# Sixteen-head attention: where the products for the row maxima stand among scores and values

## The chip, the cores and the metric

One core of one Trainium2 chip runs one program. The metric is the device time of one execution in microseconds (us), as the median of the runs. The engines: PE is TensorE (matmuls; PEld its weight loads), DVE is VectorE, ACT is ScalarE, POOL is GpSimd, SP is SyncE, which issues the DMAs here.

## The reference, cut to what matters

The program is a two-layer block on x (8 x 512 x 256) with a context of 8 x 1601 x 256. The change touches the first cross-attention alone, of 16 heads with 16 dimensions each:

```
v = (values @ Wv.T).reshape(N, -1, H, Dh)     # N = 8, 1601 keys, H = 16, Dh = 16
k = (keys @ Wk.T).reshape(N, -1, H, Dh)
q = (query @ Wq.T).reshape(N, -1, H, Dh)      # 512 queries
energy = jnp.einsum('nqhd,nkhd->nhqk', q, k)
attn = jax.nn.softmax(energy / jnp.sqrt(jnp.float32(EMBED_DIM)), axis=3)
out = jnp.einsum('nhql,nlhd->nqhd', attn, v).reshape(N, -1, H * Dh)
```

Behind it come four experts, a second attention with one wide head, and a memory layer with product keys; they stay as they are.

## The kernel before

`attend_heads` (L333) works through 32 units, `unit(b, g)` (L530): one of 8 batches, one group of four heads. The scores of a head are taken keys by queries, 128 keys at a time, so that one unit has 13 tiles of keys (`KT`) times four heads (`HG`) = 52 score products of up to 128 x 512 (`scores`, L506), as many exps on ScalarE (`exps`, L585) and as many value products (`values`, L515), which add up in one PSUM bank over the unit, each head in 32 of its partitions. Queries and keys are held as bf16 parts, six of them stacked in the rows of `qs` and `ks`, and three more rows carry minus the row's maximum, so that the exp needs no bias.

Those maxima have to be known a unit ahead. So, beside the work of unit u, TensorE computes rough scores of unit u + 1 (and, from step 10 on, of unit u + 2), queries by keys, and VectorE takes their maxima. That is `max_product` (L485), 32 jobs (`NJ`) of a pair of matmuls each, one for either head of two, with up to 401 columns; the two matmuls use rows 0 to 63 and 64 to 127 of the array. A reduction (L650) follows each pair. When all 32 are reduced, VectorE takes the maxima of the partial maxima (L654), TensorE turns them (`turn_max`, L501, called at step `TURN_AT` = 10), VectorE splits them in three bf16 parts (`split`, L632 to L640, in the order of VectorE's work ahead of reduction 0), and SP copies these into the rows of `qs` (`rows_out`, L408), which the first scores of the next unit wait for (L545). The transposed maxima lie in the second buffer of the maxima, so job 1 waits for the split (L493).

The order on each engine is written out by hand and each runs its own queue in order. On TensorE, the loop of steps (L542) goes from kt = 1 to 13: a step issues the four scores of key tile kt (in step 13 the first four of the next unit) and the four values of tile kt - 1. `plan` (L355) says at which places of a step the pairs stand: the number j means ahead of score j, so 3 is ahead of the last of the four, and `HG` = 4 is behind the last; "values" is behind the four values. Six steps (`THREE`, L351) have three pairs, the other seven two.

PSUM has eight banks: three for scores (`SBANKS`), one for the sum of the values, and two buffers of two banks for maxima (`MBANKS`). The waits that matter are two: a score waits for the exp three before it (L511), and a pair of maxima waits for the reduction of the pair two before it:

```
pe.wait_ge(m_red, u * NJ + n + 1)                 # L495; m_red starts at MBANKS = 2
```

VectorE has one more duty in the loop: the inversion of the sums of the unit before, in three pieces (`invert`, L619: a transposition L626, a reciprocal L628, a transposition L630), ahead of the reductions that `INVERT_AT` (L349) names. POOL divides with the result and spreads the values; ScalarE copies the sums out at the end of the unit (L598).

Of the kernel before, what the change touches and what calls it, by code (L numbers as in the profile page):

```python
# [28 lines left out]
KT = -(-KEYS // P)  # L29
H, DH = 16, 16  # L30
HG = 4
# [301 lines left out]
def attend_heads(nc, sem, t):  # L333
# [12 lines left out]
    SCALE = 1.0 / float(D) ** 0.5  # L346
    UNITS = B * G
    NLOAD = 2 * len(Q_PART) + 2 * MAX_PARTS
    INVERT_IN, INVERT_AT = 3, (16, 17, 21)  # L349
    TURN_AT = 10  # L350
    THREE = (1, 4, 6, 8, 11, 13)  # L351
    NJ = len(max_jobs)
    EARLY = sum(2 + (kt in THREE) for kt in range(TURN_AT, KT + 1))
    order = iter([*range(EARLY, NJ), *range(EARLY)])
    plan = {kt: {place: next(order) for place in ((2, HG, "values") if kt in THREE else (HG - 1, "values"))}  # L355
            for kt in range(1, KT + 1)}
    with Stage(nc, "at") as st:
        ks, qs = st.sb("ks", [STACK, SLOTS, HG, KEYS], BF16), st.sb("qs", [STACK, SLOTS, HG, S], BF16)
        kh, qh = st.sb("kh", [P, SLOTS, HG // 2, KEYS], BF16), st.sb("qh", [P, SLOTS, HG // 2, S], BF16)
# [24 lines left out]
        with nc.Block() as block:  # L384
# [60 lines left out]
            def _(pe):  # L445
# [39 lines left out]
                def max_product(b, g, u, n):  # L485

                    p, q, c = max_jobs[n]
                    a, w = MSPANS[c]
                    if n == 0:
                        pe.wait_ge(kq_in[g], b * 16 * NLOAD + 16 * NLOAD)  # L490
                    if n == 1:

                        pe.wait_ge(m_parts, u + 1)  # L493

                    pe.wait_ge(m_red, u * NJ + n + 1)  # L495
                    nc.tensor.matmul(ps_m[:, n % MBANKS, 0, 0:w], qs[0:MAX_ROWS, g, 2 * p, q * P:q * P + P],  # L496
                                     ks[0:MAX_ROWS, g, 2 * p, a:a + w], start=True, stop=True)
                    nc.tensor.matmul(ps_m[:, n % MBANKS, 1, 0:w], qh[MAX_ROWS:2 * MAX_ROWS, g, p, q * P:q * P + P],  # L498
                                     kh[MAX_ROWS:2 * MAX_ROWS, g, p, a:a + w], start=True, stop=True).then_inc(m_mm, 1)

                def turn_max(u):  # L501

                    pe.wait_ge(m_all, u + 1)
                    nc.tensor.transpose(turned_at, nmax[:, :], t["ident"][:, :]).then_inc(m_turned, 1)

                def scores(u, g, n):  # L506
                    kt, j = n // HG, n % HG
                    r = key_rows(kt)


                    pe.wait_ge(expd, u * NST + n + 1 + (SBANKS - 1 if g == n == 0 else 0))  # L511
                    nc.tensor.matmul(ps_s[0:r, (NST * g + n) % SBANKS, :], ks[:, g, j, kt * P:kt * P + r], qs[:, g, j, :],  # L512
                                     start=True, stop=True).then_inc(s_mm, 1)

                def values(u, g, n):  # L515
                    kt, j = n // HG, n % HG
                    r = key_rows(kt)

                    pe.wait_ge(expd, u * NST + n + 1 + SBANKS)
                    nc.tensor.matmul(ps_o[j * 32:(j + 1) * 32, :], vw[0:r, g % 2, kt * HG + j, :],  # L520
                                     pr[0:r, (NST * g + n) % PRING, :], start=kt == 0, stop=kt == KT - 1).then_inc(pv, 1)
# [8 lines left out]
                def unit(b, g):  # L530

                    u = b * G + g
                    nxt, over = ((b, x) if x < G else (b + 1, x - G) if b < last else None for x in (g + 1, g + 2))
                    def maxima(place, kt):

                        ahead, v = (nxt, u + 1) if kt < TURN_AT else (over, u + 2)
                        if place in plan[kt] and ahead is not None:
                            max_product(ahead[0], ahead[1], v, plan[kt][place])  # L540

                    for kt in range(1, KT + 1):  # L542
                        if kt == KT and nxt is not None:
                            pe.wait_ge(ones, nxt[1] + 1)
                            pe.wait_ge(m_in, u * 48 + 97)  # L545
                        for j in range(HG):
                            maxima(j, kt)
                            if kt < KT:
                                scores(u, g, kt * HG + j)
                            elif nxt is not None:  # L550
                                scores(u + 1, nxt[1], j)
                        maxima(HG, kt)
                        if nxt is not None and kt == TURN_AT:
                            turn_max(u + 1)
                        if kt == 1:
                            pe.wait_ge(v_wide, u + 1)

                            pe.wait_ge(acc_out, u + 1)
                        for j in range(HG):
                            values(u, g, (kt - 1) * HG + j)  # L560
                        maxima("values", kt)
# [6 lines left out]
                turn_max(0)  # L568
                for n in range(1, EARLY):
                    max_product(0, 1, 1, n)  # L570
                pe.wait_ge(k_out, len(halves))
                first_scores(0, 0)
                for b in range(B):
                    for g in range(G):
                        unit(b, g)
# [1345 lines left out]
def build(nc, ins, out, debug=None):  # L1921

    with ExitStack() as ctx:
# [59 lines left out]
        with nc.Block() as block:  # L1983
# [6 lines left out]
            def _(act):  # L1990
                act.wait_ge(t["consts"], 32)
                nc.scalar.activation(opened[:, :], gates[:, :], ACT.Tanh).then_inc(gates_opened, 1)
        project(nc, sem, t)
        attend_heads(nc, sem, t)
        stage_life.close()
        experts(nc, sem, t)
# [68 lines left out]
```

## Time and profile before

| | us |
|---|---|
| median of 3 runs (range) | 3662.23 (3660.39 to 3664.3) |
| the profiled execution | 3665.15 |
| its span, first to last instruction | 3663.4 |
| busy in it: TensorE matmuls | 3423.8 |
| VectorE | 2504.0 |
| ScalarE | 1513.7 |
| reductions of L650, 1024 of them | 974.3 |
| exps of L591, 1664 | 858.5 |
| scores of L512, 1664 | 524.1 |
| values of L520, 3328 (two for each value product) | 444.1 |
| maxima products, L496 and L498, 1024 each | 356.4 and 356.2 |

Matmuls are pipelined: a matmul's row may run on into the next one's, so the distance between starts, not the duration, tells what a matmul costs. In a row of the timeline a run of like instructions is merged: "x3" with 0.82 us is three, from the start of the first to the end of the last; where a stretch cuts a run, the row counts those up to the cut. What stands in brackets is the idle time of the engine ahead of the row and what ended it.

### The profile page before, as it was taken

To read this page: it belongs to the slowest core of one execution; us is meant where nothing else is said; L and a number is where in the kernel's file an instruction comes from. 1 tells how busy PE (TensorE), PEld (TensorE's weight loads), DVE (VectorE), ACT (ScalarE), POOL (GpSimd) and SP (SyncE) were. 2 spreads that over 40 slices of the span, in tenths; PEclk is the share of its full clock that TensorE was granted. 3 is DMA by queue.
4 is the path that set the end of the run, shared out by engine and by line. 5 is a ranking of instruction groups with operands and counts; after the bars stand their busy time and mean duration, and the time that the engine had idled before them with its cause. 6 is when DMAs were issued, how large, how long until landed. Compare 5 with 4: busy or idle time off the path is not lost. (4 is left out here: it accounts for less than half of the span.)

```text
span 3663.4 us, 63094 instructions
## 1 busy us (share of the span) xinstructions
PE 3423.8 (93%) x21900; PEld 2030.0 (55%) x21900; DVE 2504.0 (68%) x5808; ACT 1513.7 (41%) x2718; POOL 227.1 (6%) x251
## 2 busy tenths in 40 slices
PE   8979999999999999769977999987999999999999
PEld 5643222222222222258864545545889888989888
DVE  5538888888888888350013344438888888888885
ACT  4534777777777777512211222212222222222221
POOL 0021100000000000030000000000000000000000
PEclk9977999999999999979988999998999999999999
DMA  6687646455464552141120121212000000000000
GB/s 215 236 253 90 83 63 81 69 74 78 65 83 66 76 74 34 52 170 37 37 88 30 61 87 53 77 45 110 12 11 10 13 10 11 10 11 10 11 10 9
DMA packets 144167, 239.79 MB, mean 65 GB/s; under 512 B 22808, under 2 KB 100224, under 8 KB 143488
## 3 DMA queue, kind: packets, MB, share of 16 engines
q1 hardware_dynamic: 134768, 220.67, 28.4%
q0 software_dynamic: 4608, 12.59, 1.1%
q10 hardware_dynamic: 4624, 4.46, 0.4%
q8 instruction: 86, 1.41, 0.2%
q14 instruction: 81, 0.66, 0.1%
HBM read 170.38 MB, written 66.86 MB: 65 GB/s over the span
## 5 line engine op out<-in xcount | busy, mean ns | idle before, releaser
L650 DVE TENSOR_REDUCE at_pmax<-at_psm 128x2 f32<-128x800 f32 (+1 forms) x1024 | 974.3, 987 | 147.5 <-PE at_psm L498 128.8
L591 ACT ACTIVATE ring<-at_pss 128x512 f32<-128x512 f32 (+1 forms) x1664 | 858.5, 602 | 318.9 <-PE at_pss L512 318.9
L512 PE MATMUL at_pss<-at_qs,at_ks 99*128 99x512 bf16 (+1 forms) x1664 | 524.1, 387 | 16.8 <-ACT ring L591 8.1
L1653 PE MATMUL mt_psd<-mt_xl,mt_key_in 128*128 128x128 f32 x4096 | 491.0, 278 | 2.4 <-DMA mt_key_out<-m_out 2.4
L1653 PEld LDWEIGHTS mt_psd<-mt_xl,mt_key_in 128*128 128x128 f32 x4096 | 469.6, 193 | 3.8 <-DMA mt_key_out<-m_out 2.5
L1679 PE MATMUL mt_psu<-mt_key_out,mt_g 128*128 128x256 f32 x2048 | 447.4, 379 | 1.3 <-DVE mt_g L1889 1.3
L520 PE MATMUL at_pso<-ring,at_vw 128*32 128x512 f32 (+1 forms) x3328 | 444.1, 606 | 0.0
L496 PEld LDWEIGHTS at_psm<-at_ks,at_qs 64*128 64x128 bf16 x1024 | 95.1, 93 | 580.5 <-DVE at_pmax L650 351.3
L1679 PEld LDWEIGHTS mt_psu<-mt_key_out,mt_g 128*128 128x128 f32 x2048 | 386.7, 190 | 52.6 <-DVE mt_g L1889 1.4
L496 PE MATMUL at_psm<-at_ks,at_qs 64*128 64x400 bf16 (+1 forms) x1024 | 356.4, 348 | 20.5 <-DVE at_mpart L640 11.8
L498 PE MATMUL at_psm<-at_kh,at_qh 64*128 64x400 bf16 (+1 forms) x1024 | 356.2, 348 | 0.0
L1741 ACT ACTIVATE mt_g<-mt_psd 128x512 f32<-128x512 f32 x256 | 152.8, 597 | 351.3 <-PE mt_psd L1653 350.9
L512 PEld LDWEIGHTS at_pss<-at_qs,at_ks 99*128 99x128 bf16 (+1 forms) x1664 | 129.8, 98 | 264.5 <-ACT ring L591 154.8
L1889 DVE TENSOR_TENSOR mt_g<-mt_psc,mt_g 128x512 f32<-128x512 f32 x256 | 164.1, 683 | 55.8 <-PE mt_psc L1668 55.7
L1240 PE MATMUL aw_pss<-aw_ctxT,aw_gT 128*128 128x512 f32 (+1 forms) x512 | 187.6, 520 | 9.1 <-ACT aw_gT L1335 9.1
L1260 PE MATMUL aw_psw<-aw_pT,aw_ctx 128*128 128x512 f32 (+1 forms) x416 | 183.1, 594 | 0.8 <-issue 0.8
L1717 ACT ACTIVATE mt_sims<-mt_psx 128x512 f32<-128x512 f32 x64 | 38.2, 597 | 350.1 <-PE mt_psx L1626 350.1
L1395 DVE TENSOR_REDUCE aw_peak<-aw_pss 128x1 f32<-128x1601 f32 x32 | 58.4, 1825 | 175.9 <-PE aw_pss L1240 175.9
L1668 PEld LDWEIGHTS mt_psc<-mt_hot_w,mt_hot_m 128*128 128x128 f16 x4096 | 136.9, 98 | 36.2 <-issue 34.8
L1240 PEld LDWEIGHTS aw_pss<-aw_ctxT,aw_gT 128*128 128x128 f32 x512 | 91.3, 194 | 110.5 <-issue 98.8
L1859 DVE TENSOR_TENSOR mt_hot_m<-mt_iota_m,mt_picksT 128x2048 f16<-128x2048 f16 x128 | 150.2, 1214 | 0.0
L1357 ACT ACTIVATE aw_prob<-aw_pss,aw_shift 128x1601 f32<-128x1601 f32 x32 | 51.1, 1596 | 237.3 <-DVE aw_shift L1398 236.9
(218 smaller groups left out, 3792.3 us busy)
## 6 DMA issues: line engine op xcount, KB each, us to landing
at_ks<-k_dram SPq DMA_DIRECT2D x192, 200.1 KB, 6.7
k_dram<-pj_kp SPq DMA_DIRECT2D x24, 800.5 KB, 5.4
v_dram<-pj_v SPq DMA_DIRECT2D x8, 1664.0 KB, 9.1
at_vd<-v_dram SPq DMA_DIRECT2D x32, 416.0 KB, 10.7
pj_ctx<-ctxT SPq DMA_DIRECT2D x8, 1601.0 KB, 11.7
at_kh<-k_dram SPq DMA_DIRECT2D x128, 100.1 KB, 5.5
aw_ctxT<-ctxT SPq DMA_DIRECT2D x8, 1601.0 KB, 7.4
at_qs<-q_dram SPq DMA_DIRECT2D x192, 64.0 KB, 6.9
```

Of the source, the lines that this page charges most:

```text
L496: nc.tensor.matmul(ps_m[:, n % MBANKS, 0, 0:w], qs[0:MAX_ROWS, g, 2 * p, q * P:q * P + P], ks[0:MAX_ROWS, g, 2 * p, a:a + w], start=True, ...
L498: nc.tensor.matmul(ps_m[:, n % MBANKS, 1, 0:w], qh[MAX_ROWS:2 * MAX_ROWS, g, p, q * P:q * P + P], kh[MAX_ROWS:2 * MAX_ROWS, g, p, a:a + w] ...
L512: nc.tensor.matmul(ps_s[0:r, (NST * g + n) % SBANKS, :], ks[:, g, j, kt * P:kt * P + r], qs[:, g, j, :], start=True, stop=True).then_inc(s ...
L520: nc.tensor.matmul(ps_o[j * 32:(j + 1) * 32, :], vw[0:r, g % 2, kt * HG + j, :], pr[0:r, (NST * g + n) % PRING, :], start=kt == 0, stop=kt ...
L591: nc.scalar.activation(pr[0:r, (NST * g + n) % PRING, :], ps_s[0:r, (NST * g + n) % SBANKS, :], ACT.Exp, scale=SCALE).then_inc(expd, 1)
L650: nc.vector.tensor_reduce(pmax[:, 2 * p:2 * p + 2, q, c:c + 1], ps_m[:, n % MBANKS, :, 0:MSPANS[c][1]], AX.X, ALU.max).then_inc(m_red, 1)
L1240: ins = nc.tensor.matmul(ps_s[:, n, 0:w], gT[:, k, q * P:q * P + P], ctxT[:, s, k, a:a + w], start=k == 0, stop=k == KC - 1)
L1260: ins = nc.tensor.matmul(ps_w[:, m, :], ctx[0:r, kt, m * P:m * P + P], pT[0:r, s, kt, :], start=kt == 0, stop=kt == KT - 1)
L1653: ins = nc.tensor.matmul(ps_d[:, j % 2, y * P:y * P + P], key_in[:, k, j * YB + y, :], xl[:, s, k, :], start=k == 0, stop=k == KC - 1)
L1679: ins = nc.tensor.matmul(ps_u[:, 0:D], g[:, off % 2, y, :], key_out[:, y, :], start=y == 0, stop=y == YH - 1)
L1741: nc.scalar.activation(g[:, off % 2, j * YB:(j + 1) * YB, :], ps_d[:, j % 2, :].rearrange("p (y n) -> p y n", n=P), ACT.Gelu).then_inc(g_o ...
L1889: nc.vector.tensor_tensor(gv, ps_c[:, tb % CRING, h, :].rearrange("p (n u y) -> p y u n", u=2, y=YH), gv, ALU.mult).then_inc(w_out, 1)
```

## The change

The pairs of maxima are put at other places among scores and values, their numbers stay. Each step has two pairs back to back ahead of the third score (one in step 10), and seven steps, named in the new `THREE`, have another one behind the values. No pair stands between the scores and the values any more. With nine instead of ten pairs from step 10 on (`EARLY`), the three pieces of the inversion move by one reduction.

```diff
-    INVERT_IN, INVERT_AT = 3, (16, 17, 21)
+    INVERT_IN, INVERT_AT = 3, (17, 18, 22)
     TURN_AT = 10
-    THREE = (1, 4, 6, 8, 11, 13)
+    THREE = (2, 3, 5, 7, 8, 11, 13)
+    BETWEEN = 2
     NJ = len(max_jobs)
-    EARLY = sum(2 + (kt in THREE) for kt in range(TURN_AT, KT + 1))
+
+    def pairs_at(kt):
+
+        return {BETWEEN: 1 if kt == TURN_AT else 2, "values": int(kt in THREE)}
+
+    EARLY = sum(sum(pairs_at(kt).values()) for kt in range(TURN_AT, KT + 1))
     order = iter([*range(EARLY, NJ), *range(EARLY)])
-    plan = {kt: {place: next(order) for place in ((2, HG, "values") if kt in THREE else (HG - 1, "values"))}
-            for kt in range(1, KT + 1)}
+    plan = {kt: {place: [next(order) for _ in range(n)] for place, n in pairs_at(kt).items()} for kt in range(1, KT + 1)}
+    assert next(order, None) is None
...
                         ahead, v = (nxt, u + 1) if kt < TURN_AT else (over, u + 2)
-                        if place in plan[kt] and ahead is not None:
-                            max_product(ahead[0], ahead[1], v, plan[kt][place])
+                        if ahead is not None:
+                            for n in plan[kt].get(place, ()):
+                                max_product(ahead[0], ahead[1], v, n)
...
-                        maxima(HG, kt)
```

## Rows read from the trace of the kernel before

**Rows 1.** All scores, first and last start; busy times of one unit in steady state.
```profile
L512 PE MATMUL at_pss<-at_qs,at_ks x1664: 379/389/634, 317.6 to 1524.5; 99*128 99x512 bf16 x171, 99*65 99x512 bf16 x14
...
737.26:775.12 37.86, 37.20 (x224) 9.26 (x222) 32.99 (x40) 27.37 (x53) 2.14 (x2) 1.00 0.55 73
```
**Rows 2.** Waits in the stage: waiting line, engine waited for, total us, times, longest.
```profile
PEld at_psm L496 <- DVE at_pmax L650: 343.3, 455, 0.8
ACT ring L591 <- PE at_pss L512: 317.8, 381, 2.5
```
**Rows 3.** Timeline (start us, us) of TensorE over step 2, two pairs.
```profile
743.00 0.34 PE L496 MATMUL at_psm<-at_ks,at_qs 64*128 64x401 bf16 x1
...
743.28 0.82 PE L512 MATMUL at_pss<-at_qs,at_ks 99*128 99x512 bf16 x3
744.03 0.34 PE L496 MATMUL at_psm<-at_ks,at_qs 64*128 64x400 bf16 x1
...
744.42 0.39 PE L512 MATMUL at_pss<-at_qs,at_ks 99*128 99x512 bf16 x1
744.74 1.06 PE L520 MATMUL at_pso<-ring,at_vw 128*32 128x512 f32 x8
745.74 0.34 PE L496 MATMUL at_psm<-at_ks,at_qs 64*128 64x400 bf16 x1
...
746.01 0.39 PE L512 MATMUL at_pss<-at_qs,at_ks 99*128 99x512 bf16 x1
```
**Rows 4.** Timeline of ScalarE, the first exp of step 2.
```profile
743.77 0.60 ACT L591 ACTIVATE ring<-at_pss 128x512 f32<-128x512 f32 x1 [0.94 <-PE at_pss L512]
```
**Rows 5.** Timeline of TensorE, the first half of step 1, three pairs.
```profile
740.27 0.61 PE L512 MATMUL at_pss<-at_qs,at_ks 99*128 99x512 bf16 x2
740.81 0.34 PE L496 MATMUL at_psm<-at_ks,at_qs 64*128 64x400 bf16 x1
...
741.09 0.71 PE L512 MATMUL at_pss<-at_qs,at_ks 99*128 99x512 bf16 x2
```
**Rows 6.** Timeline of VectorE, cut behind one reduction (twice) and behind two.
```profile
743.39 0.99 DVE L650 TENSOR_REDUCE at_pmax<-at_psm 128x2 f32<-128x802 f32 x1 [0.22 <-PE at_psm L498]
...
731.03 0.97 DVE L650 TENSOR_REDUCE at_pmax<-at_psm 128x2 f32<-128x802 f32 x1
...
731.03 1.87 DVE L650 TENSOR_REDUCE at_pmax<-at_psm 128x2 f32<-128x802 f32 x2
```
**Rows 7.** Timeline of TensorE, steps 10 and 11, with the turn of the maxima.
```profile
728.12 0.82 PE L512 MATMUL at_pss<-at_qs,at_ks 99*128 99x512 bf16 x3
...
729.53 0.28 PE L504 MATMUL at_psm<-ident_sb,at_nmax 128*16 128x128 f32 x1
729.74 1.06 PE L520 MATMUL at_pso<-ring,at_vw 128*32 128x512 f32 x8
731.16 0.34 PE L496 MATMUL at_psm<-at_ks,at_qs 64*128 64x400 bf16 x1 [0.35 <-DVE at_mpart L640]
...
731.43 0.61 PE L512 MATMUL at_pss<-at_qs,at_ks 99*128 99x512 bf16 x2
732.06 0.34 PE L496 MATMUL at_psm<-at_ks,at_qs 64*128 64x400 bf16 x1
...
734.50 0.41 PE L512 MATMUL at_pss<-at_qs,at_ks 99*65 99x512 bf16 x1
```
**Rows 8.** Timeline of VectorE in step 10, the maxima of the partial maxima.
```profile
729.26 0.22 DVE L654 TENSOR_REDUCE at_nmax<-at_pmax 128x16 f32<-128x64 f32 x1
```
**Rows 9.** Timeline of VectorE, reductions around the first two pieces of the inversion.
```profile
747.15 0.99 DVE L650 TENSOR_REDUCE at_pmax<-at_psm 128x2 f32<-128x800 f32 x1
...
748.88 0.99 DVE L650 TENSOR_REDUCE at_pmax<-at_psm 128x2 f32<-128x802 f32 x1
...
750.16 0.99 DVE L650 TENSOR_REDUCE at_pmax<-at_psm 128x2 f32<-128x800 f32 x1
```
**Rows 10.** The splits' row DMAs (L413), 60 of them, issue to landing.
```profile
DMA to landing us min/median/max: 1.7/1.8/2.1
```

## The prediction

> **What bounds the kernel now.** The change touches one stage, the 16-head attention, so I read that stage alone. The row of all scores gives its extent, 317.6 to 1524.5 us: 32 units (one batch, four heads) of about 37.7 us, and the row of one unit shows TensorE busy 37.20 of 37.86 us, VectorE 32.99, ScalarE 27.37, at a granted clock of 1.00 [rows 1]. That looks like a unit full of TensorE work. It is not: busy is modelled and overlapping there. The list of waits says that the maxima's weight loads wait for VectorE (343.3 us) and ScalarE waits for scores (317.8 us) [rows 2]. The first of these misleads as well, since most of that idle time of the weight port is time in which the matmul port runs the values. So I went to single instructions, over one step of each kind.
>
> Call the four scores of a step S0 to S3, the four values V, a pair of maxima products M. A step of two pairs, from S0 to the next S0 [rows 3]: S0 at 743.28, S3 at 744.42 (+1.14), V at 744.74 (+0.32), M at 745.74 (+1.00), S0 at 746.01 (+0.27), in all 2.73. The 1.14 is a chain: three score banks, so S3 needs the exp of S0. That exp starts 0.49 after S0 and takes 0.60 [rows 4], and S3 follows 0.05 later. The first pair sits inside this 1.14 and costs nothing; the pair behind the values costs 0.27. A step of three has one more pair between S3 and V, 0.28 more: 740.27 to 743.28 is 3.01 [rows 5 and 3]. VectorE never holds TensorE up in these steps. A reduction starts 0.39 behind its pair (743.00, 743.39) and lasts 0.99 [rows 3, 6], so that of the pair behind V is over 1.11 after S0; the closest pair that wants its bank, the one between S3 and V in a step of three, starts at 1.14 + 0.32 = 1.46. The reserve is 0.35. One unit is then five steps of 3.01 (13, 1, 4, 6, 8), five of 2.73 (2, 3, 5, 7, 9), the step of the turned maxima, 10, at 3.31, step 11 at 3.07 [rows 7], and step 12 at 2.76 (734.50 to 737.26, the start of the unit's row): 37.85, against 37.86 in [rows 1].
>
> **What the change moves.** No instruction is added or removed: 32 pairs per unit (12 x 2 + 1 + 7; the new assertion says so too, which leaves no room for a change that does something else), 52 scores, 52 values, the same reductions. Their order on TensorE becomes S0 S1 M M S2 S3 V, and in steps 2, 3, 5, 7, 8, 11, 13 one more M behind V; step 10 has one M in all. VectorE's three pieces of the inversion stand ahead of reductions 17, 18 and 22 in place of 16, 17 and 21. No DMA moves past another on SP's queue, and POOL's queue is as it was.
>
> **Spacings, start to start.** S0 to the first M 0.54, M to S 0.28 [rows 5]; S to S 0.22 (a run of three lasts 0.82, of which the last has 0.39), S3 to V 0.32, V to M 1.00, M to S0 0.27 [rows 3]. Not in the trace is M to M where nothing holds the second. Two scores in a row hide their weight load and follow at 0.22 for 512 columns, which makes 0.17 for 400; with the load exposed, as between M and S, it is 0.28. I take 0.17, by the scores, the only rows of one shape behind itself; the other end adds 0.1 to two steps in the unit, 6 us in all. The Trainium skill, TensorE: Matmul & The Clock Gate, Part 3, The mechanism, says that a weight load overlaps matmuls in flight only where the row group differs; by that the gap would be 0.28 and the sum 6 us more; the scores, all in the same rows and 0.22 apart, do not agree with it. V to S0 without a pair between isn't there either: 1.00, as V to M; with the load hidden it could be 0.9, in six steps of the unit, 18 us less in all.
>
> **What the new order costs.** The maxima have two buffers, so a pair needs the end of the reduction of the pair two before it. In a step that follows one with a pair behind V, the second of the two pairs ahead of S2 needs just that pair's reduction. It begins 0.39 after its M, lasts 0.99, and the waiting pair starts 0.06 after it (a reduction from 731.03 for 0.97, the pair at 732.06) [rows 6, 7]. So the second M comes 1.44 after the M behind V, which is 1.17 after S0, in place of 0.71. Behind it on TensorE's queue stand S2, S3 and V: +0.28, +0.22, +0.32, +1.00, together 1.82. That makes four kinds of step:
> - free, two pairs: 0.54 + 0.17 + 1.82 = 2.53 (S3 at 1.21, so the exp chain of 1.14 is just covered); free, three: 2.80.
> - blocked, two: 1.17 + 1.82 = 2.99; blocked, three: 3.26.
>
> Now the unit. Seven of the thirteen steps stand right behind a step of three and are blocked: 1, 3, 4, 6, 8, 9 and 12. Free are only 2 and 13, both of three pairs. Step 5 would be free, but the first two pieces of the inversion now fall into step 4: with the transposition between, the reductions are 1.73 apart (747.15, 748.88), with the reciprocal 1.28 (750.16) [rows 9]. In step 4 they start (counted from its S0) at 0.12, 1.85 and 3.13, the last ends at 4.12, and the second M of step 5 starts at 4.18, 1.19 after its S0 (2.99): 1.19 + 1.82 + 0.27 = 3.28. The third piece, again a transposition, in step 6: reductions at 0.12, 1.85 and 2.75 (0.90 apart, 731.03 twice, 1.87 for two less 0.97 for one [rows 6]), end at 3.74, pair at 3.80, against 2.99 + 0.71 free: step 7 is 2.80 + 0.10 = 2.90.
>
> Step 10 gains. Now: turn at +1.41, V 0.21 later, then the second pair waits for the split of the turned maxima until 731.16, 1.63 after the turn [rows 7]. After: S3 1.14, turn 1.41, V 1.62, S0 of step 11 at 2.62; step 11's first pair comes 1.75 after the turn, past the 1.63. The turn itself isn't late: the last reduction of step 9 ends at 1.17 + 0.39, put back to 1.92 by the one before, + 0.99 = 2.91, the reduction of all (0.22 [rows 8]) by 3.2, and the turn comes at 2.99 + 1.41. Step 11: reduction 0 starts 1.50 after the turn, lasts 0.97, so the second pair starts at turn + 2.53, 1.32 after S0; 1.32 + 1.82 + 0.27 = 3.41.
>
> Sum of steps 1 to 9: 2.99, 2.80, 3.26, 2.99, 3.28, 2.99, 2.90, 3.26, 2.99 = 27.46; before 25.70. Steps 10 to 13: 2.62, 3.41, 2.99, 2.80 = 11.82; before 3.31 + 3.07 + 2.76 + 3.01 = 12.15. The unit: 39.28 against 37.86 (37.85 by the sum), **1.42 us more**. Thirty units have all their maxima: 42.6. The last but one has steps 1 to 9 only, +1.8; the last has none. Ahead of the first unit one pair less is done, -0.9. Together +43.5 us.
>
> What hides the rest: the splits' three row DMAs must have landed by the S0 of step 13, 6.0 us after the split's end (6.2 now), and they land 1.7 to 2.1 us from issue [rows 10]. ScalarE's four exps, 0.60 each [rows 4], need 2.4 us at most, less than any step. The granted clock is 1.00 and TensorE stays as busy, so I leave it.
>
> The profiled execution is 3665.15 us (span 3663.4, 1.75 around it), 2.9 above the median of 3662.23; the sum gives 3708.6 for a like execution, and on the median 3705.7.
>
> **Rivals.** (A) Blocked, as above: 3706, chance 0.80. For it: [rows 7], where a pair waits for its reduction and the two scores behind it wait too.
> (B) The second pair isn't held up, faster. Then a unit is five steps of 2.53, seven of 2.80 and 2.62: 34.87, 2.99 less, 3570 in all. It would be so if a reduction let go of its bank 0.46 sooner, so that the second M starts 0.71 after S0; below a shortening by 0.16 in each of the nine held-up steps the change still loses (1.42 / 9). A release at the end of the reading rather than the writing would bring about 0.09 (0.99 against a pace of 0.90 [rows 6]), which isn't enough. Against: the end that releases is measured. Chance 0.10. The Trainium skill, Perfetto Trace Analysis, Optimizing Tensor Performance, Matmuls, says that independent groups should rotate through PSUM banks so that the evacuation of one overlaps the matmuls of the next; the two pairs do so, and by that rule alone this rival would hold. The trace's wait at 732.06 is that very rotation, come round too soon.
> (C) The stalls are there but each some 0.16 smaller, and the gain at V, S0 and step 10 makes up for it: 3662, within 0.2%; chance 0.05.
> (D) The stalls spread (two three-pair steps in a row, 2 and 3, 7 and 8, leave VectorE behind by one reduction more, 0.9 per unit): 3733; chance 0.05.
>
> **The numbers.** Central 3706. The unknowns give -18 (load hidden behind V), -4 (a reduction of 0.97) and +6 (M to M): 3684 to 3712; a little of D on top: 3684 to 3718, which holds about 0.80. This kernel's time can be told from no change at about 0.2%, 7 us; A and D are slower, 0.84 with what is near them, C same 0.05, B and what is between faster 0.11.
>
> **What would show it.** The unit at 39.3 us from S0 to S0; steps 1, 4, 6, 9 and 12 at 2.99, 3 and 8 at 3.26, 5 at 3.28, and none at 2.53; the second pair 1.44 behind the pair after V; S2 0.28 behind it; step 10 at 2.62. The waits for the reduction on the pair's line should have matmul idle time, which they now have only in step 11. I am wrong if steps of 2.5 appear (B), if two maxima run more or less than 0.17 to 0.28 apart where free, or if the change in the stage isn't the change in the total.

## The result

| | us |
|---|---|
| before, median | 3663.27 (3660.39 to 3664.42) |
| changed, median | 3697.10 (3695.71 to 3699.13) |
| ratio, 95% interval | 1.0093 (1.0077 to 1.0109) |
| changed, the profiled execution and its span | 3699.13, 3697.5 |

Slower by 33.8 us, where 43.5 were forecast: the right side and the right mechanism, and a forecast nearly three tenths above what was measured. The profiled executions differ by 34.0 us (3665.15 to 3699.13). All of it lies in the stage: from the first score to the last it took 1206.9 us before (317.6 to 1524.5 [rows 1]) and takes 1242.2 now, and it begins 0.9 us earlier. The same views of the changed kernel, first all scores, then a unit (stretch, length, busy TensorE, weight port, VectorE, ScalarE, POOL, clock, DMA share, GB/s), then two waits between 330 and 1550 us (line, engine waited for, total us, times, longest; the list counts idle times over 0.15 us):

```profile
L518 PE MATMUL at_pss<-at_qs,at_ks x1664: 376/389/634, 316.7 to 1558.9; 99*128 99x512 bf16 x171, 99*65 99x512 bf16 x14
```

```profile
709.64:748.64 39.00, 36.31 (x226) 8.26 (x222) 32.53 (x40) 28.35 (x54) 2.15 (x2) 1.00 0.56 71
```

```profile
ACT ring L597 <- PE at_pss L518: 325.6, 651, 1.0
...
PE at_psm L502 <- DVE at_pmax L656: 82.0, 274, 0.5
```

The unit is 39.00 against 37.86 [rows 1], and TensorE is busy 36.31 of it against 37.20: its new time is idle time. This is a unit of the usual length. Six units before and eight now are 0.2 to 0.4 longer, and the mean of 29 grows by 1.14 as well; the first unit grew by 1.01 and the last but one by 1.28, which makes the stage's 35.3. The last row is the new one. In the list of before no such row was among the waits of the matmul port in the stage (the pair of step 11 waited 0.02 us per unit, too short for the list); now 274 pairs, nine in each of some thirty units, wait 82.0 us in all for the reduction that holds their buffer. The row of the weight port, which looked alarming before (343.3 [rows 2]), is 341.9 now: it told nothing either time.

Where that wait stands, in step 9, which follows a step of three (timeline: start us, duration us), on TensorE:

```profile
736.43 0.34 PE L502 MATMUL at_psm<-at_ks,at_qs 64*128 64x400 bf16 x1
...
736.71 0.61 PE L518 MATMUL at_pss<-at_qs,at_ks 99*128 99x512 bf16 x2
737.25 0.34 PE L502 MATMUL at_psm<-at_ks,at_qs 64*128 64x400 bf16 x1
...
737.87 0.34 PE L502 MATMUL at_psm<-at_ks,at_qs 64*128 64x400 bf16 x1 [0.28 <-DVE at_pmax L656]
...
738.14 0.61 PE L518 MATMUL at_pss<-at_qs,at_ks 99*128 99x512 bf16 x2
738.68 1.06 PE L526 MATMUL at_pso<-ring,at_vw 128*32 128x512 f32 x8
739.68 0.39 PE L518 MATMUL at_pss<-at_qs,at_ks 99*128 99x512 bf16 x1
```

and on VectorE:

```profile
736.82 0.99 DVE L656 TENSOR_REDUCE at_pmax<-at_psm 128x2 f32<-128x800 f32 x1 [0.46 <-PE at_psm L504]
```

The pair behind the values starts at 736.43, its reduction runs from 736.82 to 737.81, and the second pair of step 9 starts 0.06 later, at 737.87: 1.44 behind 736.43 and 1.16 behind S0 at 736.71. The two scores and the values queue behind it, and the step, from S0 to S0, takes 2.97 us. In [rows 3], with the same number of pairs, it was 2.73.

Nothing holds the second pair in step 2, which follows a step of two:

```profile
715.40 0.60 PE L518 MATMUL at_pss<-at_qs,at_ks 99*128 99x512 bf16 x2
715.94 0.34 PE L502 MATMUL at_psm<-at_ks,at_qs 64*128 64x400 bf16 x1
...
716.12 0.33 PE L502 MATMUL at_psm<-at_ks,at_qs 64*128 64x401 bf16 x1
...
716.39 0.39 PE L518 MATMUL at_pss<-at_qs,at_ks 99*128 99x512 bf16 x1
```

The two pairs are 0.18 apart, and S2 follows 0.27 behind the second.

### The profile page after: what moved, and what is told of

The parts are those of the page before. It is cut to its first block and busy times, and to the rows that moved or that the text cites. A ratio compares the mean times of both kernels' runs of the same rounds, so it can differ in the third digit from the quotient of the medians.

```text
span 3697.5 us, 63094 instructions
## 1 busy us (share of the span) xinstructions
PE 3396.2 (92%) x21900; PEld 1999.0 (54%) x21900; DVE 2489.7 (67%) x5808; ACT 1544.3 (42%) x2718; POOL 227.7 (6%) x251
## 5 line engine op out<-in xcount | busy, mean ns | idle before, releaser
L656 DVE TENSOR_REDUCE at_pmax<-at_psm 128x2 f32<-128x800 f32 (+1 forms) x1024 | 961.9, 985 | 161.4 <-PE at_psm L504 143.8
L597 ACT ACTIVATE ring<-at_pss 128x512 f32<-128x512 f32 (+1 forms) x1664 | 888.6, 595 | 331.0 <-PE at_pss L518 330.7
L518 PE MATMUL at_pss<-at_qs,at_ks 99*128 99x512 bf16 (+1 forms) x1664 | 510.4, 387 | 7.3 <-ACT ring L597 6.5
L502 PE MATMUL at_psm<-at_ks,at_qs 64*128 64x400 bf16 (+1 forms) x1024 | 340.3, 347 | 91.3 <-DVE at_pmax L656 85.0
L504 PE MATMUL at_psm<-at_kh,at_qh 64*128 64x400 bf16 (+1 forms) x1024 | 340.1, 347 | 0.0
L518 PEld LDWEIGHTS at_pss<-at_qs,at_ks 99*128 99x128 bf16 (+1 forms) x1664 | 108.2, 98 | 324.8 <-ACT ring L597 208.8
L526 PEld LDWEIGHTS at_pso<-ring,at_vw 128*32 128x32 f32 (+1 forms) x3328 | 65.8, 108 | 157.8 <-ACT ring L597 101.5
```

The costliest lines, as they stand in the source:

```text
L597: nc.scalar.activation(pr[0:r, (NST * g + n) % PRING, :], ps_s[0:r, (NST * g + n) % SBANKS, :], ACT.Exp, scale=SCALE).then_inc(expd, 1)
L656: nc.vector.tensor_reduce(pmax[:, 2 * p:2 * p + 2, q, c:c + 1], ps_m[:, n % MBANKS, :, 0:MSPANS[c][1]], AX.X, ALU.max).then_inc(m_red, 1)
```

## The experiments

Every time below has a ratio to the kernel before, measured on the same chip with it: its median was 3666.95 us for the first four rows and 3663.66 for the last three, so times of different chips are compared by their ratios. Unit lengths are from S0 to S0 of a usual unit, in us.

| label | what | us | ratio (95%) | unit |
|---|---|---|---|---|
| half_after | changed, reductions over half the columns (half of the scores is left out of the maxima) | 3581.51 | 0.9771 (0.9755 to 0.9788) | 35.18 |
| half_before | before, the same | 3659.50 | 0.9980 (0.9971 to 0.9990) | 37.74 |
| hg_after | changed, held second pairs behind S3 | 3660.28 | 0.9981 (0.9971 to 0.9991) | 37.70 |
| turn_before | before, one pair in step 10 | 3650.99 | 0.9958 (0.9941 to 0.9975) | 37.38 |
| inv_after | changed, inversion later | 3682.72 | 1.0052 (1.0038 to 1.0066) | 38.51 |
| alternate | steps of three and two in turn | 3627.98 | 0.9904 (0.9889 to 0.9920) | 36.70 |
| alternate_11 | the same, step 11 too | 3614.31 | 0.9869 (0.9853 to 0.9884) | 36.30 |

**Is it the length of the reduction?** The reduction is shortened and the order left alone, in the changed kernel and, as its control, in the one before. The end of the reduction's line, what it reads:

```diff
-    ps_m[:, n % MBANKS, :, 0:MSPANS[c][1]],
+    ps_m[:, n % MBANKS, :, 0:MSPANS[c][1] // 2],
```

> The changed kernel with every reduction of the maxima reading only the left half of its columns (half of the scores is left out of the maxima); order, matmuls and waits stay. My theory: the second pair of a step is held by the reduction of the pair behind the values; at about 0.57 us instead of 0.99 that reduction ends 0.75 after S0, where the pair could start at 0.71 anyway, so steps 1, 4, 6, 9, 12 fall to about 2.55, steps of three to 2.8, the unit from 39.0 to about 35.2 us and the kernel to about 3582. Rival: two pairs back to back cost by themselves (weight loads, scores that reach ScalarE in bursts); then nothing changes, 3697.

> The kernel before with the same halved reductions (half of the scores is left out of the maxima). My theory: in the old order VectorE holds TensorE only in steps 10 and 11, so the unit falls by 0.1 us or less, the kernel stays within 5 us of 3663. Rival (the reductions are the bound in both orders): it falls like the changed kernel, by about 100 us.

Step 1 of half_after, which follows a step of three (TensorE, VectorE, and the row of a unit):

```profile
712.15 0.34 PE L502 MATMUL at_psm<-at_ks,at_qs 64*128 64x400 bf16 x1
...
712.43 0.61 PE L518 MATMUL at_pss<-at_qs,at_ks 99*128 99x512 bf16 x2
712.96 0.34 PE L502 MATMUL at_psm<-at_ks,at_qs 64*128 64x400 bf16 x1
...
713.17 0.34 PE L502 MATMUL at_psm<-at_ks,at_qs 64*128 64x400 bf16 x1
```

```profile
712.54 0.58 DVE L656 TENSOR_REDUCE at_pmax<-at_psm 128x2 f32<-128x400 f32 x1 [0.92 <-PE at_psm L504]
```

```profile
704.28:739.63 35.35, 35.22 (x225) 8.82 (x222) 19.84 (x40) 27.82 (x54) 2.15 (x2) 1.00 0.58 79
```

The reduction lasts 0.58 and ends at 713.12, and the second pair starts at 713.17, 0.74 behind S0, where 0.75 was expected (as the end of the reduction, by a slip; it is the start of the pair). TensorE has 0.13 us of idle time left in the unit shown, the usual unit is 35.18 (this one has 0.17 more), and the time is 3581.5, or 3579.4 by its ratio on the scale of the result, against 3582 expected. In the order of before the same cut brings 0.12 us per unit. The ratio of half_before is 0.9980, 7 us (4 to 11 by the interval), where at most 5 were expected; the stage is 3.1 us shorter, and the rest is not explained. So the reduction's length costs TensorE 3.8 us per unit in the new order and 0.12 in the old; pairs back to back cost next to nothing by themselves, and the new order would be the better one with short reductions, which is rival (B) with its condition met. That shorter reductions speed up both orders alike is ruled out by half_before.

**Is it the place of the second pair?** Only the second pair of the seven steps behind a step of three moves, to between S3 and the values.

```diff
-        return {BETWEEN: 1 if kt == TURN_AT else 2, "values": int(kt in THREE)}
+        between = 1 if kt == TURN_AT or (kt - 1 or KT) in THREE else 2
+        behind = 2 - between if kt != TURN_AT else 0
+        return {BETWEEN: between, HG: behind, "values": int(kt in THREE)}
...
+                        maxima(HG, kt)
                         if nxt is not None and kt == TURN_AT:
                             turn_max(u + 1)
```

> The changed kernel, but in the seven steps that follow a step of three pairs, the second of the two pairs stands between the fourth score and the values, not back to back with the first. My theory: there it starts 1.46 after S0, past the end of the reduction it needs, and S3 is back on its exp at 1.14, so these steps fall from 2.97 to 2.74 and from 3.25 to 3.01; step 5 grows by 0.25, since reduction 18 still stands behind two pieces of the inversion; unit 37.7, kernel about 3657, level with the kernel before or a little faster. Rival (the third pair behind the values is what costs): nothing comes back, 3697.

Step 8 and, in the last row, the second pair of step 5, on TensorE; then what is left of the wait, and the unit:

```profile
756.18 0.34 PE L504 MATMUL at_psm<-at_ks,at_qs 64*128 64x400 bf16 x1
...
757.00 0.34 PE L504 MATMUL at_psm<-at_ks,at_qs 64*128 64x400 bf16 x1
...
757.92 0.34 PE L504 MATMUL at_psm<-at_ks,at_qs 64*128 64x401 bf16 x1
...
758.19 1.07 PE L528 MATMUL at_pso<-ring,at_vw 128*32 128x512 f32 x8
...
748.73 0.34 PE L504 MATMUL at_psm<-at_ks,at_qs 64*128 64x401 bf16 x1 [0.55 <-DVE at_pmax L659]
```

```profile
PE at_psm L504 <- DVE at_pmax L659: 29.5, 60, 0.6
```

```profile
733.23:770.93 37.70, 36.71 (x225) 8.82 (x222) 32.51 (x41) 27.70 (x53) 2.15 (x2) 1.00 0.56 73
```

At 757.92 the pair comes 1.74 behind the pair behind the values (756.18), past the 1.44 it needs, and waits for nothing. The waits in the list fall from nine to two per unit (60), those of steps 5 and 11. Steps of two went from 2.97 to 2.73, of three from 3.25 to 3.01. Step 5 grew to 3.52 as expected: its second pair needs reduction 18, which stands behind two pieces of the inversion and whose own pair now comes later. Step 7 grew from 2.79 to 2.90, which was not expected: there the reduction ends 0.06 ahead of a second pair that comes 0.28 behind the first in place of 0.18, so this pair is held by 0.1 as well, too short a wait for the list. All the loss and a little more is back, with the third pairs still behind the same values: the rival, that these cost, falls.

**What is the inversion's part?**

```diff
-    INVERT_IN, INVERT_AT = 3, (17, 18, 22)
+    INVERT_IN, INVERT_AT = 3, (19, 22, 24)
```

> The changed kernel with the three pieces of the inversion ahead of reductions 19, 22 and 24 instead of 17, 18 and 22. My theory: step 5 is long (3.28) only because two pieces stand in step 4 ahead of the reduction that its second pair needs; here the first piece runs in idle time of VectorE at the start of step 5 and the third at the start of step 7, so step 5 is 2.80, the other steps stay, unit 38.5, kernel 15 us less than the changed one (3682 on its scale). Rival (the pieces are too short to matter beside reductions, step 5 is long for another reason): 3697, step 5 stays 3.28.

Step 5 in inv_after (TensorE), and the first piece (VectorE):

```profile
757.47 0.34 PE L502 MATMUL at_psm<-at_ks,at_qs 64*128 64x400 bf16 x1
...
757.65 0.33 PE L502 MATMUL at_psm<-at_ks,at_qs 64*128 64x401 bf16 x1
```

```profile
756.77 0.70 DVE L632 STREAM_TRANSPOSE quad<-quad 128x512 f32<-128x512 f32 x1
757.85 0.99 DVE L656 TENSOR_REDUCE at_pmax<-at_psm 128x2 f32<-128x800 f32 x1 [0.38 <-PE at_psm L504]
```

The transposition now lies in idle time, with 0.38 us of it left, the second pair of step 5 starts 0.18 behind the first, and step 5 is 2.79 in place of 3.28. The other steps are unchanged. Unit 38.51, time 14.4 us below that of the change (15.0 by the ratios), 15 expected. That is 0.49 of the unit's 1.14: over two fifths of the loss depend on where the pieces stand. Whether they would have cost less if the change had left them ahead of 16, 17 and 21 was not run; by the order of the pairs, the first would then delay the reduction of the pair behind the values of step 3, for which step 4 waits. It isn't a separate cause, though. The pieces cost because they lengthen the time until the buffer comes free; in the order of before the first two stretch the reductions by as much [rows 9], and steps 3, 4 and 5 take 2.73, 3.01 and 2.73 there, as the other steps of two and three pairs do.

**Does step 10 gain?** One part of the change alone, on the kernel before:

```diff
-    THREE = (1, 4, 6, 8, 11, 13)
+    THREE = (1, 4, 6, 8, 11, 12, 13)
...
-    EARLY = sum(2 + (kt in THREE) for kt in range(TURN_AT, KT + 1))
+    EARLY = sum(2 + (kt in THREE) - (kt == TURN_AT) for kt in range(TURN_AT, KT + 1))
...
-    plan = {kt: {place: next(order) for place in ((2, HG, "values") if kt in THREE else (HG - 1, "values"))}
+    plan = {kt: {place: next(order) for place in ((2, HG, "values") if kt in THREE else (HG - 1,) if kt == TURN_AT else (HG - 1, "values"))}
```

> The kernel before with one part of the change alone: one pair in step 10, the one behind its values moved to step 12, which gets three; all else stays. My theory: step 10 falls from 3.31 to 2.6, step 11 from 3.07 to 3.01, step 12 grows from 2.76 to 3.03; unit 0.5 us less, kernel 3647. Rival (the wait for the split only moves to the next pair): unit +0.25, kernel 3671.

The turn and the start of step 11 in turn_before (TensorE), and a unit:

```profile
763.61 0.28 PE L504 MATMUL at_psm<-ident_sb,at_nmax 128*16 128x128 f32 x1
763.82 1.06 PE L520 MATMUL at_pso<-ring,at_vw 128*32 128x512 f32 x8
764.82 0.39 PE L512 MATMUL at_pss<-at_qs,at_ks 99*128 99x512 bf16 x1
```

```profile
733.48:770.86 37.38, 37.13 (x223) 9.25 (x222) 32.97 (x40) 27.38 (x53) 2.14 (x2) 1.00 0.58 74
```

Step 11 begins 1.21 behind the turn, as the sum had it, where it began 1.90 behind it before (729.53 to 731.43 [rows 7]). Step 10 is 2.62, step 11 3.01, step 12 3.03, the unit 0.48 shorter, the kernel 0.42% faster. This is the part of the change that is sound; on the chip of this comparison it is 16 us below the kernel before, and the rival, that the wait for the split only moves, falls.

**The parts put together.** If the account is right, an order can be written down in which no pair waits: back to back pairs only in steps that no pair behind values precedes, steps of three and two in turn, the pieces of the inversion where VectorE idles, and in step 11 the second pair past the split. The step of hg_after is used with

```diff
-    INVERT_IN, INVERT_AT = 3, (17, 18, 22)
+    INVERT_IN, INVERT_AT = 3, (16, 21, 26)
...
-    THREE = (2, 3, 5, 7, 8, 11, 13)
+    THREE = (2, 4, 6, 8, 9, 11, 13)
```

for alternate, and for alternate_11 with one line more:

```diff
-        between = 1 if kt == TURN_AT or (kt - 1 or KT) in THREE else 2
+        between = 1 if kt in (TURN_AT, TURN_AT + 1) or (kt - 1 or KT) in THREE else 2
```

> Steps of three (two pairs back to back, one behind the values) at 2, 4, 6, 8, 9, 11, 13, so that but for 9 each is followed by a step of two whose pairs stand ahead of S2 and behind S3 (9: one ahead of S2, one behind S3, one behind the values); inversion pieces ahead of 16, 21 and 26. My theory: no pair waits for a reduction except in step 11: steps of three 2.80, steps of two 2.74, step 9 3.01, step 10 2.57, step 11 3.41, unit 36.6; kernel about 3623 on the scale of 3663 for the one before (ratio 0.989). Rival (hg_after's gain came from having fewer pairs back to back, and back to back costs elsewhere): unit 37.7 or more, no faster than hg_after.

> As the one before, and in step 11 the second pair stands behind S3. My theory: step 11 falls from 3.41 to 3.01, since reduction 0, which begins only behind the split, is over 1.32 after S0 and the pair comes at 1.46; unit 36.2, kernel about 3611 on the scale of 3663 (ratio 0.986). Rival (step 11 is held by the split itself): it stays 3.4, 3623.

Steps 1 and 2 of alternate_11, from the pair behind the values of step 13 on, and its unit:

```profile
721.23 0.34 PE L504 MATMUL at_psm<-at_ks,at_qs 64*128 64x401 bf16 x1
...
721.51 0.61 PE L520 MATMUL at_pss<-at_qs,at_ks 99*128 99x512 bf16 x2
...
722.97 0.34 PE L504 MATMUL at_psm<-at_ks,at_qs 64*128 64x400 bf16 x1
...
724.25 0.60 PE L520 MATMUL at_pss<-at_qs,at_ks 99*128 99x512 bf16 x2
...
724.96 0.33 PE L504 MATMUL at_psm<-at_ks,at_qs 64*128 64x401 bf16 x1
...
727.04 0.39 PE L520 MATMUL at_pss<-at_qs,at_ks 99*128 99x512 bf16 x1
```

```profile
718.71:755.02 36.31, 36.31 (x226) 8.85 (x222) 32.55 (x41) 27.41 (x53) 2.15 (x2) 1.00 0.61 77
```

Step 1 takes 2.74, step 2, with three pairs, 2.79, and no wait of the matmul port for a reduction is in the list of this kernel's stage. Unit 36.30, of which VectorE works 32.55. The pair that is now behind S3 in step 11 brings 0.40 per unit (the step goes from 3.40 to 3.01), as expected, so the step was held by reduction 0 and not by the split. Both kernels came 0.1 us per unit, 3 to 5 us in all, above the expected sums, and this is a slip of adding: the steps named in the expectation of alternate make 36.69 and not 36.6, and 36.70 was measured; less 0.40 they make 36.29, and 36.30 was measured. Within the sum, steps 10 and 12 take 2.62 and 2.76 instead of 2.57 and 2.74, and most others 0.01 less than expected. The better of the two is 1.3% faster than the kernel before and 2.2% faster than the change.

## Why the prediction was right, and by how much it was off

- **The bound.** That TensorE's queue order with its waits, not anyone's busy time, sets the unit: right. In half_after VectorE's work per unit drops from 32.5 to 19.8 and in half_before from 33.0 to 21.0; the order with blocked pairs gains 3.8 us per unit from it, the other 0.12.
- **The second pair held for 1.44.** Measured 1.44 in step 9, and 0.06 after the reduction's end, as read from one wait in step 11 of the kernel before. Nine steps of the unit were forecast as held by a full wait (1, 3, 4, 5, 6, 8, 9, 11 and 12) and step 7 by 0.10; 274 waits in some thirty units are the nine, and step 7 is not held.
- **Kinds of step.** Forecast and measured: blocked of two 2.99 and 2.97, blocked of three 3.26 and 3.25, free of three 2.80 and 2.79 or 2.80, step 5 3.28 and 3.28, step 11 3.41 and 3.41. Free steps of two are absent from the change, as forecast. In half_after steps of two are 2.55 against 2.53, of which 0.03 is still a hold (its pairs are 0.21 apart and not 0.18).
- **What was mis-sized.** The unit grew by 1.14 and not by 1.42. Of the 0.28, 0.11 is step 7 (2.90 forecast, 2.79 measured): I gave the third piece of the inversion the price of the first, 1.73 from reduction to reduction. In the program only the first and the second have a wait for their own result behind them, before anything else may start. The rows of VectorE in steps 4 and 6:

```profile
721.55 0.99 DVE L656 TENSOR_REDUCE at_pmax<-at_psm 128x2 f32<-128x802 f32 x1 [0.46 <-PE at_psm L504]
722.46 0.70 DVE L632 STREAM_TRANSPOSE quad<-quad 128x512 f32<-128x512 f32 x1
723.29 0.99 DVE L656 TENSOR_REDUCE at_pmax<-at_psm 128x2 f32<-128x800 f32 x1
724.20 0.24 DVE L634 RECIPROCAL at_inv<-quad 128x16 f32<-128x16 f32 x1
724.56 0.99 DVE L656 TENSOR_REDUCE at_pmax<-at_psm 128x2 f32<-128x800 f32 x1
...
727.81 0.99 DVE L656 TENSOR_REDUCE at_pmax<-at_psm 128x2 f32<-128x800 f32 x1 [0.46 <-PE at_psm L504]
728.72 0.70 DVE L636 STREAM_TRANSPOSE quad<-at_inv 128x512 f32<-128x512 f32 x1
729.34 1.85 DVE L656 TENSOR_REDUCE at_pmax<-at_psm 128x2 f32<-128x800 f32 x2
```

  With the same 0.70 us of transposition, reductions are 1.74 apart around the first and 1.53 around the third. Another 0.05 is step 10, 2.57 for 2.62: the turn follows S3 by 0.22, where I took 0.27 from the order of before. Those 0.27 held a wait for VectorE that I took for a spacing: before, the reduction over the partial maxima ended at 729.48 [rows 8], and the turn started 0.05 behind it, at 729.53 [rows 7]. In the change that reduction ends before S1, and the turn goes right behind S3, which starts at 740.82 (VectorE, then TensorE from S2 on):

```profile
739.64 0.22 DVE L660 TENSOR_REDUCE at_nmax<-at_pmax 128x16 f32<-128x64 f32 x1
...
740.49 0.72 PE L518 MATMUL at_pss<-at_qs,at_ks 99*128 99x512 bf16 x2
741.04 0.27 PE L510 MATMUL at_psm<-ident_sb,at_nmax 128*16 128x128 f32 x1
```

  In alternate and alternate_11 the reduction is as late as before, and step 10 takes 2.62 again. The remaining 0.12 is in steps that each came out 0.01 to 0.02 shorter, all on one side. S3 to V, 0.31 in the change where I took 0.32 from steps in which S3 waits for an exp, makes about as much over twelve steps; the second decimals of the other distances go either way. Over the 29 whole units, 0.28 makes 8.1 of the 9.5 us that the forecast is high; 0.4 is the first unit (1.01 more and not 1.42), 0.5 the last but one (1.28 and not 1.8), and some 0.4 lie outside the stage.
- **Luck in the range.** 3697.1 lies in the stated range only thanks to the 18 us at its low end, set aside for a weight load hidden behind V, and that load was not hidden. The terms that were too large, the third piece and the turn, had no allowance; without the 18 us the range would have begun at 3702.
- **The unknown gaps.** M to M without a wait is 0.18, near the end I took (0.17) and far from the 0.28 that I had worked out for a load that is not hidden. By the rule of the Trainium skill (TensorE: Matmul & The Clock Gate, Part 3, The mechanism), that a load overlaps matmuls in flight only where the row group differs, it would not be hidden; the trace does not agree with it: in step 2 of the change the second pair's loads run from 715.95 to 716.05, while the first pair's matmuls, in the same rows, run from 715.94 to 716.28. V to S0 without a pair is 1.00 (738.68 to 739.68), as taken; the 18 us kept for a hidden load were not there.
- **Rivals.** (B) needed a buffer free 0.46 sooner. half_after made it so (by 0.41) and got 3581.5, against the 3570 of (B). Its unit is 35.18 against 34.87, and 0.19 of the 0.31 is step 11 (2.99 for 2.80), where the second pair waits for the split and reduction 0 even so; (B) had left that out. (C), holds 0.16 smaller each, did not occur: the blocked steps are within 0.02 of the forecast. (D), a backlog from adjacent steps of three, did not occur either: steps 3 and 8 are both 3.25. The rule of rotation of the Trainium skill (Perfetto Trace Analysis, Optimizing Tensor Performance, Matmuls), that independent groups rotate through banks so that the evacuation of one overlaps the matmuls of the next, is enough in this kernel only where the rotation is slower than a buffer's round, 1.44 us from pair to pair of one buffer.
- **Slips without weight.** The steps printed for the kernel before add up to 37.84 and not 37.85, and the reserve of 0.35 leaves out the 0.06 of the release, so it was 0.29.

## What to carry to other kernels

With two buffers, what counts is the distance in time between every other use, not that the uses alternate: write down for each place the time since the use before last, and compare it with product, reduction and release, here 1.44 us. Work that is hidden in the middle of one chain (in a free step, two pairs ahead of S2 put S3 at 1.21, only 0.07 behind the 1.14 that its exp allows) may still be too early for another, and because the engine's queue is in order the wait is paid by everything behind it. An order of 13 steps could be costed by hand from start-to-start distances: to 0.3 us per unit for the change, and to less than 0.1 for the five orders of the experiments, the slip in adding put right. A start-to-start distance taken from an old order may contain a wait, as that of the turn did. The better order followed from the same table.

## What the runs showed of the hardware

Two things I had not expected. The 0.70 us of a transposition on VectorE cost the stream of reductions 0.63 or 0.84 (1.53 or 1.74 less the 0.90 without one), and the program waits for its own result behind the dearer one only. The reciprocal, which has such a wait too, ends at 724.44, 0.12 ahead of the next reduction, as the first transposition does (723.16 to 723.29), while the reduction behind the third piece starts 0.08 before that ends; this fits, but no run takes the wait alone out. And a reduction over half the elements lasts 0.58 instead of 0.99, so, by an estimate from these two, some 0.17 of it does not shrink with its length.
